# Attention scores in a macaron block: fp32 matmuls written as three fp32r products of high and low parts

## The reference

```python
x = x + 0.5 * ffn(layernorm(x), w1, b1, w2, b2)      # gelu, 1024 hidden units
x = x + attn(layernorm(x), w_qkv, w_out, b_out)
x = x + 0.5 * ffn(layernorm(x), w1, b1, w2, b2)

q, k, v = heads(x @ w_qkv)
sim = (q * 64 ** -0.5) @ k.T - slope[h] * abs(j - i)  # j > i masked out
out = heads_joined(softmax(sim) @ v) @ w_out + b_out
```

## Time and profile before

| | |
|---|---|
| Time, median of 3 runs | 2198.57 us (2197.63 to 2198.59) |
| The profiled execution | 2198.49 us |
| its span, first to last instruction | 2196.7 us |
| TensorE busy | 2144.5 us, 98% |
| its weight loads | 1741.3 us, 79% |
| VectorE busy | 1506.4 us, 69% |
| ScalarE busy | 1234.8 us, 56% |
| GpSimd busy | 1070.2 us, 49% |
| mean granted TensorE clock | 0.991 of full |

### The profile page before, as it was taken

How to read it: one execution, slowest core, us unless ns; L and a number is a source line. 1 busy time by engine, 2 the same in 40 slices (tenths; PEclk the granted TensorE clock), 3 DMA queues, 4 the chain that set the end, 5 groups by cost and what they waited for, 6 DMA issues and landing times.

```text
span 2196.7 us, 41801 instructions
## 1 busy us (share of the span) xinstructions
PE 2144.5 (98%) x14720; PEld 1741.3 (79%) x14720; DVE 1506.4 (69%) x4011; ACT 1234.8 (56%) x3096; POOL 1070.2 (49%) x1773
## 2 busy tenths in 40 slices
PE   5999999999999999999999999999999999999998
PEld 5678787887878778787887878878787787878866
DVE  7666766758676676766767667686766767667664
ACT  4654736557364564646547365573646646465471
POOL 3653826537174462735538265371744627355371
PEclk8999999999999999999999999999999999999998
DMA  3331504325052340513415043250523405133151
GB/s 129 103 100 36 152 26 127 86 64 137 13 143 70 85 128 8 157 49 106 107 34 154 25 125 88 65 139 10 146 67 87 126 9 156 49 107 106 34 144 35
DMA packets 109985, 193.91 MB, mean 88 GB/s; under 512 B 34512, under 2 KB 53200, under 8 KB 109776
## 3 DMA queue, kind: packets, MB, share of 16 engines
q1 hardware_dynamic: 89296, 138.77, 22.5%
q0 software_dynamic: 20480, 52.47, 9.7%
HBM read 14.95 MB, written 8.39 MB: 11 GB/s over the span
## 4 chain that ended last, share of the span: by engine, by line
PE 87%; ACT 4%; POOL 4%; DVE 3%; issue 1%; SPq 1%; DMA 0%; DVEq 0%; POOLq 0%; ACTq 0%
PE ps L283 85%; POOL P L942 3%; ACT P L604 2%; PE ps L337 2%; ACT L604 1%; DVE P L787 1%; SPq L229 1%; ACT qk L564 1%; DVE x L734 0%; DVE gl L705 0%; POOL PT L229 0%; DVE gh L754 0%; DMA raw<-in_L_ffn_w 0%; DMA PT<-P 0%; DVE xtl L705 0%
## 5 line engine op out<-in xcount | busy, mean ns | idle before, releaser
L942 POOL TENSOR_SCALAR P<-P,rs 128x512 f32<-128x512 f32 (+3 forms) x1024 | 540.8, 547 | 439.0 <-DVE rs L770 435.6
L604 ACT ACTIVATE P<-P,mx 128x512 f32<-128x512 f32 (+3 forms) x1024 | 562.5, 552 | 196.6 <-DVE mx L779 196.5
L229 POOL DMA_DIRECT2D PT<-P x640 | 322.7, 509 | 240.9 <-DVE P L787 222.4
L787 DVE STREAM_TRANSPOSE P<-P 128x1792 f32<-128x1792 f32 (+1 forms) x256 | 374.0, 1485 | 12.4 <-POOL P L942 11.8
L283 PE MATMUL ps<-qk 64*128 64x512 f32 (+3 forms) x2048 | 312.2, 444 | 4.5 <-ACT qk L564 4.5
L283 PE MATMUL ps<-PT,v 128*64 128x256 f32 (+1 forms) x3072 | 307.9, 350 | 6.1 <-DMA PT<-P 3.8
L283 PE MATMUL ps<-w2h,gh 128*128 128x256 f32 x1024 | 294.7, 288 | 6.6 <-DVE gl L705 6.4
L283 PE MATMUL ps<-w2l,gh 128*128 128x256 f32 x1024 | 290.9, 284 | 0.0
L283 PE MATMUL ps<-w2h,gl 128*128 128x256 f32 x1024 | 290.7, 284 | 0.0
L283 PEld LDWEIGHTS ps<-PT,v 128*64 128x64 f32 x3072 | 205.0, 138 | 103.4 <-issue 13.2
L564 ACT ACTIVATE qk<-ps 128x512 f32<-128x512 f32 x256 | 153.0, 598 | 231.7 <-PE ps L283 231.7
(11 more groups left out here) (83 smaller groups left out, 4411.6 us busy)
## 6 DMA issues: line engine op xcount, KB each, us to landing
PT<-P SPq DMA_DIRECT2D x1408, 80.0 KB, 2.6
PT<-P POOLq DMA_DIRECT2D x640, 80.0 KB, 2.7
x<-in_L_attn_x SPq DMA_DIRECT2D x16, 512.0 KB, 4.3
out_y<-x SPq DMA_DIRECT2D x15, 512.0 KB, 3.2
raw<-in_L_ffn_w SPq DMA_DIRECT2D x2, 512.0 KB, 5.9
raw<-in_L_ffn_w SPq DMA_DIRECT2D x1, 1024.0 KB, 8.6
rawq<-in_L_attn_w_qkv SPq DMA_DIRECT2D x1, 1024.0 KB, 6.7
rawk<-in_L_attn_w_qkv SPq DMA_DIRECT2D x1, 1024.0 KB, 8.8
```

The costliest lines, as they stand in the source:

```text
L229: e.dma_start(PT[c % 2][32 * m:32 * m + 32, g, :], P[c % 3][32 * g:32 * g + 32, m, :]).then_inc(landed[c % 3].sem, 16)
L604: e.activation(p, p, ACT.Exp, bias=mx[:, r, i:i + 1], scale=-1.0, accum_out=sm[:, r, i:i + 1]).then_inc(s_ex.sem, 1)
L787: e.transpose(p, p).then_inc(s_tr.sem, 1)
L942: e.tensor_scalar(p, p, rs[:, 2 * (c % 2) + h, i:i + 1], 1.0, ALU.mult, ALU.mult).then_inc(s_nz.sem, 1)
```

## The change

Scores are no longer one fp32 matmul for each head and query block. ScalarE copies queries and keys from PSUM into an fp32 tile `qkf`, the keys now reordered on the way so that the matmul reads them in runs. When both are there, a second copy on ScalarE (128x1024) rounds them to the high part `qkh`, and VectorE subtracts it to make the low part `qkl` (`qk_lo`, in the place of `qkf`). TensorE then does three products for each head and block, the two heads taking turns, and accumulates them in PSUM.

There is one `qkh` for all pairs, so the copies of a pair wait for the scores of the pair before, where they waited for those two before. The subtraction for pair c+1 stands in VectorE's program between block 0 and block 1 of pair c; for pair 0 it stands behind the second layer norm of the first sequence, or ahead of the residues of the third layer norm of the sequence before. Of the next sequence's statistics, the first two tiles move to the ends of pairs 2 and 3. Of the sixteen transfers SP now starts ten and GpSimd six.

```diff
-    qk = [place(f"qk{i}", [128, 2, T], F32, QK + 4096 * i) for i in range(2)]
+    qkh = place("qkh", [128, 2, T], F32R, QK)
+    qkf = [place(f"qkf{i}", [128, 2, T], F32, a) for i, a in enumerate((PP + 10240, QK + 4096))]
+    qkl = [place(f"qkl{i}", [128, 2, T], F32R, a) for i, a in enumerate((PP + 10240, QK + 4096))]
...
-    SPREAD_SP, SPREAD_POOL = GROUPS[:11], GROUPS[11:]
+    SPREAD_SP, SPREAD_POOL = GROUPS[:10], GROUPS[10:]
...
             def scores(b, c):
-                e.wait_ge(s_pc.sem, s_pc.at((b, ("q", c))))
+                e.wait_ge(s_kl.sem, s_kl.at((b, c)))
+                lo = qkl[min(c, 1)]
                 for i in QORDER:
-                    w = 128 * (i + 1)
                     for h in range(2):
...
-                        hs = slice(64 * h, 64 * h + 64)
-                        keys = qk[c % 2][hs, 1, 0:w].rearrange("p (j m s) -> p m j s", m=4, s=32)
-                        mm(score_block(h, i), qk[c % 2][hs, 0, i * 128:i * 128 + 128], keys,
-                           True, True).then_inc(s_qk.sem, 1)
+                    for n, (q, k) in enumerate(((qkh, qkh), (qkh, lo), (lo, qkh))):
+                        for h in range(2):
+                            hs = slice(64 * h, 64 * h + 64)
+                            keys = k[hs, 1, :].rearrange("p (m n) -> p m n", m=4)[:, :, 0:32 * (i + 1)]
+                            last = mm(score_block(h, i), q[hs, 0, i * 128:i * 128 + 128], keys, n == 0, n == 2)
+                            if n == 2:
+                                last.then_inc(s_qk.sem, 1)
...
-                    if n >= 2:
-                        e.wait_ge(s_qk.sem, s_qk.at((*pairs[n - 2], QORDER[-1], 1)))
-                    dst = qk[c % 2][:, 0 if kind == "q" else 1, :]
+                    if n >= 1:
+                        e.wait_ge(s_qk.sem, s_qk.at((*pairs[n - 1], QORDER[-1], 1)))
+                    if kind == "q":
+                        dst = qkf[min(c, 1)][:, 0, :]
+                    else:
+                        dst = qkf[min(c, 1)][:, 1, :].rearrange("p (m j s) -> p j m s", m=4, s=32)
+                        src = src.rearrange("p (j m s) -> p j m s", m=4, s=32)
                 e.activation(dst, src, ACT.Copy).then_inc(s_pc.sem, 1)
+                if tile[0] == "q":
+                    e.wait_ge(s_pc.sem, s_pc.at((b, tile)))
+                    e.activation(qkh[:, :, :], qkf[min(c, 1)][:, :, :], ACT.Copy).then_inc(s_kh.sem, 1)
...
+            def qk_lo(b, c):
+                e.wait_ge(s_kh.sem, s_kh.at((b, c)))
+                n = min(c, 1)
+                residue(qkl[n][:, :, :], qkf[n][:, :, :], qkh[:, :, :]).then_inc(s_kl.sem, 1)
...
                 if b > 0:
                     gelu_split(2, b - 1, range(NM))
+                qk_lo(b, 1)
+                if b > 0:
                     add3(b - 1, 0)
                 inverse(b, 0, 1)
...
                     add3(b - 1, 2)
+                qk_lo(b, 2)
                 inverse(b, 1, 1)
...
                     biased(b, c, 0)
+                    if c + 1 < NC:
+                        qk_lo(b, c + 1)
                     biased(b, c, 1)
                     inverse(b, c, 1)
-                    if more and c == 4:
-                        e.wait_ge(s_x.sem, s_x.at(b + 1))
-                        for t in range(NT):
+                    if more and 2 <= c <= 4:
+                        if c == 2:
+                            e.wait_ge(s_x.sem, s_x.at(b + 1))
+                        for t in {2: [0], 3: [1], 4: [2, 3]}[c]:
                             stats(1, b + 1, t)
-                        variance(1, b + 1)
+                        if c == 4:
+                            variance(1, b + 1)
...
                 for t in range(NT):
                     normal(3, b, t)
+                if more:
+                    qk_lo(b + 1, 0)
                 ln_lo(3, b, 0)
```

More of the change, by code:

```diff
@@ L158, in build @@
     s_oa = Signal("out_copied", pairs)
+    s_kh = Signal("qk_hi", pairs)
+    s_kl = Signal("qk_lo", pairs)
     s_lh = Signal("lh_done", units)
@@ L188, in build @@
     s_y = Signal("y_out", list(B), 16)
-    s_pt = [Signal(f"spread{i}", [(b, c) for b, c in pairs if c % 3 == i], 11 * 16) for i in range(3)]
-    s_pp = [Signal(f"spread_pool{i}", [(b, c) for b, c in pairs if c % 3 == i], 5 * 16) for i in range(3)]
+    s_pt = [Signal(f"spread{i}", [(b, c) for b, c in pairs if c % 3 == i], 10 * 16) for i in range(3)]
+    s_pp = [Signal(f"spread_pool{i}", [(b, c) for b, c in pairs if c % 3 == i], 6 * 16) for i in range(3)]
     names = ["w1a", "w1b", "b1", "w2", "b2", "wq", "wk", "wv", "wout", "bout"]
@@ L891, in _ @@
                 ln_lo(2, 0, u)
+            qk_lo(0, 0)
             e.wait_ge(s_id.sem, s_id.at("dist"))
```

## The result

The change made the kernel slower: 2318.6 us (median of four runs, 2315.0 to 2320.3) against 2198.4, a ratio of 1.0545 (95% interval 1.0527 to 1.0563). I had predicted 2203, in a range of 2183 to 2218. The profiled execution took 2320.3 us, with a span of 2318.5; its mean granted clock is 0.978, against 0.991 before.

The account below looks back on a forecast made before the run. TensorE is 98% busy, but a GpSimd-VectorE loop of 9.02 us a pair was to set the pace in pairs 2 to 6. Sum: 2198.5 - 1.5 + 4.5 - 0.6 + 2 = 2202.9, say 2203 us; range 2183 to 2218.

Parts of the forecast that it names:

- the late turn of pair 5: VectorE's subtraction overruns 0.65 us spare at pair 5; turn about 0.45 late, TensorE 0.2 late at the stage's end.
- Score block: TensorE's scores of a head pair: three fp32r products take 2.13 us instead of 2.36, gaining 0.23 a pair.
- The high-part copy on ScalarE: ScalarE's 1.05 us copy per pair fits its idle 44%; exponentials start later while GpSimd still issues transfers; cost nothing.
- Inside the loop it is covered: VectorE's 1.22 us subtraction per pair is hidden: 4.7 us of VectorE work against the 6.1 GpSimd needs.
- The loop of 9.02: GpSimd and VectorE's pair-to-pair chain grows from 8.52 to 9.02 us by one 0.50 transfer, setting the pace in pairs 2 to 6.
- the first rival: GpSimd and VectorE's pair-to-pair chain has unseen slack, so TensorE's saving shows: 2176 us, partly so up to 2194; chance 0.22.
- The start: At a sequence's start, scores of pair 1 wait for copy and subtraction: 0.16 us lost.
- First sequence: Nothing covers copy and subtraction there: 2.27 us added, once more for pair 1, +4.5 in all.
- Last: In the last sequence TensorE waits 2.65 us for transfers; one SP issue fewer takes off 0.6 (0 to 1.2).
- GpSimd's stops: GpSimd's transfer issue stops six times, 13.4 us in all; perhaps seven after the change, +2 us (0 to 17).
- The load of x: Statistics moved to pair 2 wait on VectorE for a load landing after 3.7 us: usually nothing, 0.5 in a bad sequence.

Follow-up runs that it names:

- eleven: The changed kernel with SP starting eleven transfers and GpSimd five, as before the change: 2267.7 us, ratio 1.0319 to the kernel before.
- no_lo_eleven: The changed kernel without the subtraction, scores multiplying high parts three times, ScalarE's copy kept, eleven transfers on SP: 2219.9 us.
- products_only: The changed kernel without high-part copy and subtraction: ScalarE writes PSUM straight into `qkh`, three products on high parts, eleven transfers on SP: 2180.0 us.
- both: The changed kernel with eleven transfers on SP and GpSimd's addition of b2 waiting for the subtraction of pair 0: 2233.6 us, ratio 1.0164.
- no_block: The changed kernel with the next sequence's variance moved to pair 4 and normalisation to pairs 5 and 6, where GpSimd issues transfers: 2306.6 us.
- hold_bias: The changed kernel with GpSimd's addition of b2 (layer 3) waiting until VectorE's subtraction of pair 0 is done: 2278.4 us, ratio 1.0365.

## Why the prediction was wrong, step by step

In the prediction's own terms: ScalarE's copy, put at nothing, costs 39.9 us; the subtraction, taken as covered, costs 47.8; and the late turn of pair 5, sized at 0.45 with 0.2 left for TensorE, starts 3.5 us later behind the scores of pair 2 than before (42.3 against 38.8, means of the fourteen middle sequences), and only 0.4 later in eleven.

The ladder prices each part, in us: three products 18.5 off; the copy to the high parts 39.9 on (no_lo_eleven over products_only); the subtraction 47.8 (eleven over no_lo_eleven), of which 34.1 go with GpSimd's addition held back (both over eleven); the sixth transfer 50.9 (the changed kernel over eleven). The sum is 120.1.

*Score block*: right, and not by luck. 2.11 against 2.13; a middle step of 384 columns takes 0.18 (0.174 in the sum) and one of 128 takes 0.11 (0.120). The halves run side by side in fp32r: 3072 weight loads of 64 rows, 197 ns each, are busy for 309 us of their 605, as in the earlier trace rows:

```profile
L287 PEld LDWEIGHTS ps<-qkl,qkh 64*128 64x128 f32 x1024 | 103.3, 198 | 5.9
...
L287 PEld LDWEIGHTS ps<-qkh,qkl 64*128 64x128 f32 x1024 | 103.3, 198 | 6.0
...
L287 PEld LDWEIGHTS ps<-qkh 64*128 64x128 f32 x1024 | 102.4, 196 | 50.0 <-DVE qkl L719 28.4 <-issue 13.2
```

*"The high-part copy on ScalarE ... lies in its idle 44%"*: the first step that failed. The idle share did not cover it: what stands behind the copy in ScalarE's program is late by 1.06 us, and from there two chains lead to a bank that TensorE waits for, in the projections of pair 2 (through the addition x) and in pair 6 (through the values' copy). Of what is queued behind the copy I had looked only at the exponentials of the pairs in between, for which GpSimd is indeed still issuing.

*"Inside the loop it is covered"*: the second. For GpSimd's first four normalisations it held: in pairs 3 to 7 of the changed kernel they start right behind the six transfers (1248.52 above). The cover is thin, since they also need the reciprocal behind the subtraction: with five transfers they wait 0.3 us for it (eleven). What failed is what the sum left out. Outside the loop, at pair 0, the 1.22 from the earlier trace rows did not hold: beside GpSimd's addition it is 2.91, fifteen times of fifteen, and 34.1 of the 47.8 go with that. And behind the subtraction the variance and the normalisation start at another time against GpSimd's four, with the durations shown above.

*The loop of 9.02 sets the pace in pairs 2 to 6*: half right. From pair 2 to pair 3 the turns start 9.01 us apart, as the sum has it (mean of the fourteen middle sequences; with five transfers, in eleven, 8.79); then 10.4 and 11.1, with variance and normalisation in between. But TensorE's scores in pairs 2 to 4 come 8.8 to 9.0 apart, as the first rival had it: the values of a pair stand behind the scores of the second pair after it, and a turn that falls behind by 0.2 a pair does not show there at once. The sixth transfer's own 0.50 us is 6.5 us in the whole run; its 50.9 arise with the subtraction. no_block shows that the late projections of pairs 5 and 6 go when variance and normalisation stand elsewhere; it does not show that this gives the time back.

*Pair 5 hands on 0.45, and 0.2 is left at the end of the stage*: the overrun was there, but the normalisation itself took 3.78 instead of 2.15, on top of the 0.57, and the lateness reached TensorE at once, through ScalarE's copies, in pair 6; in pair 5 the variance had done the same. The end of the stage, where I had it show, is as before (8.76 for its down blocks, 8.74 before).

*The start*: the wait of scores 1 was 0.16 and came out as 0.24. What stands behind the subtraction of pair 0 (the residue and its bank) I had not followed: 2 us a sequence, and with it low clock.

*First sequence*: mis-sized, 15.4 for 4.5. The latency shows three times, in scores 0, 1 and 2 (their blocks start 3.8, 8.7 and 12.2 later than before), with the scores of pairs 0 and 1 at the lower clock (blocks of 3.82, granted clock 0.50). *Last*: +2.2 for -0.6; no run separates it. *GpSimd's stops*: right, six again, 16.2 us for 13.4. *The load of x*: the times of the earlier trace rows are of loads and stores together; the loads alone took 3.95 to 4.91 us. It mattered little: VectorE waited for them in four sequences of the changed kernel, 4.5 us in all.

Part of the loss is clock. With the two levels only, 1 - 0.978 and 1 - 0.991 of the spans make 102 us at 1.2 GHz against 40, so at most 31 us of the 120 are matmuls at half pace; they follow the waits (products_only 0.989, hold_bias 0.983).

Left open: how much of the 50.9 each collision carries, and where the 13.7 of the subtraction's 47.8 arise that do not go with GpSimd's addition. A version that keeps subtraction and loop but can't collide was not found; no_block only moved the wait.

## What to carry to other kernels

Price an added instruction by its place: list what is queued behind it on its engine and which banks and buffers that frees; the engine's idle share (44% here) did not tell. Take a duration from a row only with a look at the group's shortest and longest, and at what GpSimd does at the new place. And split a change that gives work to three engines into a ladder of runs: here each step looked harmless in the prediction, and two of them (0.50 us of GpSimd, 1.22 of VectorE) cost 6.5 and 47.8 us alone and 98.7 together (the changed kernel over no_lo_eleven).

## What the hardware showed

Some operations of VectorE take far longer beside GpSimd. Groups by line of the changed kernel (shortest, median, longest ns), of hold_bias, and of the kernel before:

```profile
L719 DVE TENSOR_TENSOR qkl<-qkf,qkh x128: 1211/1225/2915, 62.6 to 2248.6; 128x1024 fp32r<-128x1024 f32 x128
```

```profile
L719 DVE TENSOR_TENSOR x3l<-ps,x3h x32: 682/691/693, 193.4 to 2246.4; 128x512 fp32r<-128x512 f32 x32
```

```profile
L728 DVE TENSOR_SCALAR xn<-x,mv,rstd x192: 375/408/2040, 9.0 to 2165.7; 128x256 f32<-128x256 f32 x192
```

The subtraction with both inputs in SBUF stretches to 2.4 times. The residue x3l, with one input in PSUM, never does, though in hold_bias all 32 of them run beside one of GpSimd's additions (one is in the rows there: 0.68 at 1163.50). The longest normalisation of 2.04 us was in the trace of before, and I had read only the mean.

The Trainium skill (SBUF — State Buffer, Who interferes with whom) has a rule for this: a VectorE instruction with two SBUF inputs contends with a GpSimd instruction that reads SBUF, one with at most one SBUF input and outside the two-port modes does not, and in a two-port mode, which `tensor_scalar` can enter, whoever issues first keeps the shared ports for the whole instruction while the other is blocked. The trace agrees on the subtraction, which starts behind GpSimd's addition and ends 1.08 us after it, and takes 1.22 when the addition is held back, and on the residue. The records as they stand do not bear out the last part: the second normalisation starts at 1258.61, 0.21 us ahead of the first of GpSimd's four (0.13 when the overlap of its record with the one before is taken off), and still takes 2.84, to the end of all four, while in eleven the four of VectorE and the four of GpSimd take turns (2.38 and 2.65 us). Which of the two happens changed with 0.2 to 0.3 us in the start; why is not shown, nor in which mode these instructions ran.
